# Multiplying constants before the gathered rows arrive, in two mixture-of-experts stages

## The reference

```python
def _L0_ffn_ref(x, ...):            # E = 32 experts, K = 4 per token, at most 320 rows each
    w, idx = _gate(xf, wg)
    xe = xp[buf_tok].reshape(E, cap, DIM)              # rows gathered by expert
    h = silu(einsum('ecd,edh->ech', xe, w1)) * einsum('ecd,edh->ech', xe, w3)
    out = einsum('ech,ehd->ecd', h, w2) * buf_w
    y = zeros.at[buf_tok].add(out)                     # rows sent home
    z = silu(xf @ sw1) * (xf @ sw3) @ sw2              # shared expert, every token
    return y + z

def _L3_ffn_ref(x, ...):            # 7 routed experts, 2 per token, one shared; hidden 512
    routed_out = _swiglu(x_flat, w_gate, w_up, w_down)
    mixed = einsum('end,ne->nd', routed_out, combine)
    return mixed + mean(_swiglu(x_flat, sw_gate, sw_up, sw_down), axis=0)
```

## Time and profile before

| | us |
|---|---|
| median of 3 runs | 1672.77 |
| lowest and highest | 1665.45, 1678.71 |
| profiled execution | 1683.69 |
| its span, first to last instruction | 1681.4 |
| TensorE busy | 1254.4 (75%) |
| VectorE busy | 1045.1 (62%) |
| ScalarE busy | 676.6 (40%) |
| GpSimd busy | 656.7 (39%) |

### The profile page before, as it was taken

How to read it: one execution, slowest core, us unless ns; L and a number is a source line. 1 busy time by engine, 2 the same in 40 slices (tenths; PEclk the granted TensorE clock), 3 DMA queues, 4 the chain that set the end, 5 groups by cost and what they waited for, 6 DMA issues and landing times.

```text
span 1681.4 us, 24800 instructions
## 1 busy us (share of the span) xinstructions
PE 1254.4 (75%) x9098; PEld 792.9 (47%) x9098; DVE 1045.1 (62%) x1915; ACT 676.6 (40%) x1275; POOL 656.7 (39%) x657
## 2 busy tenths in 40 slices
PE   5457777513777368878878559997998999965997
PEld 2123333311444134444446524454666666854996
DVE  7899999871211498878743454546665665642775
ACT  2744343210334137767741235554334234321442
POOL 1277878567366360000003330024641441043453
PEclk9679889856888579999968789998999999986998
DMA  6247567111232441211001141115000000001113
GB/s 221 103 161 258 212 233 267 55 43 49 70 81 67 151 145 39 64 57 44 16 15 31 44 154 54 38 35 220 1 1 1 1 1 1 1 31 40 37 47 95
DMA packets 75448, 133.84 MB, mean 80 GB/s; under 512 B 12723, under 2 KB 39670, under 8 KB 74688
## 3 DMA queue, kind: packets, MB, share of 16 engines
q1 hardware_dynamic: 66400, 115.97, 20.8%
q0 software_dynamic: 8064, 13.87, 2.6%
q10 hardware_dynamic: 864, 2.43, 0.4%
HBM read 96.22 MB, written 38.38 MB: 80 GB/s over the span
## 4 chain that ended last, share of the span: by engine, by line
PE 47%; issue 19%; DVE 13%; POOL 8%; ACT 5%; SPq 3%; DMA 3%; another core or an unknown queue 2%; POOLq 0%; DVEq 0%; ACTq 0%
PE ps L1840 6%; POOL sb_arena L1044 5%; PE ps L3956 3%; DVE sb_arena L1906 3%; PE ps L2207 2%; ACT sb_arena L2154 2%; PE ps L2190 2%; PE ps L2449 2%; PE ps L3115 2%; SPq L68 1%; PE ps L3131 1%; PE ps L658 1%; PE ps L3923 1%; PE ps L3924 1%
## 5 line engine op out<-in xcount | busy, mean ns | idle before, releaser
L1906 DVE TENSOR_REDUCE sb_arena<-ps 128x2 f32<-128x1024 f32 (+2 forms) x192 | 211.0, 1130 | 58.2 <-PE ps L2435 33.7
L2154 ACT ACTIVATE sb_arena<-ps 128x512 f32<-128x512 f32 (+1 forms) x320 | 160.3, 554 | 57.9 <-PE ps L2207 54.4
L658 PE MATMUL ps<-sb_arena,sb_const 128*128 128x512 f32 x256 | 136.1, 677 | 27.9 <-DVE sb_arena L852 27.9
L846 DVE TENSOR_TENSOR_SCAN sb_arena<-ps,sb_arena 128x1024 f32<-128x1024 f32 x64 | 145.0, 2279 | 4.0 <-ACT ps L945 3.1
L1938 POOL CAST sb_arena<-sb_arena 128x8 bf16<-128x8 f32 (+2 forms) x32 | 6.5, 203 | 289.4 <-DVE sb_arena L1906 148.8
L1840 PE MATMUL ps<-sb_arena 128*32 128x256 f32 (+3 forms) x1856 | 117.2, 361 | 0.2 <-ACT sb_arena L2388 0.2
L1566 POOL DMA_INDIRECT y<-sb_arena x80 | 77.7, 972 | 61.1 <-ACT sb_arena L1515 41.1
L658 PEld LDWEIGHTS ps<-sb_arena,sb_const 128*128 128x128 f32 x256 | 55.9, 220 | 93.1 <-issue 53.5
L1143 POOL DMA_INDIRECT xe<-sb_arena x80 | 78.5, 981 | 51.8 <-issue 29.2
L1044 POOL TENSOR_TENSOR sb_arena<-sb_Wreg,sb_arena 128x1024 f32<-128x1024 f32 x32 | 78.0, 2458 | 40.4 <-DMA sb_arena<-bcrows 32.2
L3776 POOL TENSOR_TENSOR sb_arena<-sb_arena 128x512 f32<-128x512 f32 x32 | 40.7, 1271 | 124.5 <-DVE sb_arena L3380 124.5
(11 more groups left out here) (519 smaller groups left out, 3233.7 us busy)
## 6 DMA issues: line engine op xcount, KB each, us to landing
sb_arena<-bcrows SPq DMA_DIRECT2D x80, 512.0 KB, 6.4
xe<-sb_one SPq DMA_DIRECT2D x31, 260.0 KB, 8.9
sb_Wreg<-e0w SPq DMA_DIRECT2D x24, 256.0 KB, 7.1
sb_arena<-xe SPq DMA_DIRECT2D x16, 325.0 KB
y<-sb_zero SPq DMA_DIRECT2D x20, 256.0 KB, 6.9
sb_arena<-y SPq DMA_DIRECT2D x4, 1024.0 KB, 9.3
sb_Wreg<-e1w SPq DMA_DIRECT2D x16, 256.0 KB, 2.7
sb_Wreg<-e3gu SPq DMA_DIRECT2D x1, 4096.0 KB, 12.5
```

Of the source, the lines that this page charges most:

```text
L658: t = e.matmul(k.b(self.Y + c), k.c("ident"), self.hc[i % 4][:, c * 512:(c + 1) * 512], start=False, stop=n == 15)
L846: e.tensor_tensor_scan(self.hh[i % 3], k.pair(2 * (i % 2)).rearrange("p c t -> p (c t)"), self.dB[i % 3], 0.0, MUL, ADD).then_inc(S.scan.s ...
L1906: e.tensor_reduce(dst, src, AX.X, MAX).then_inc(S.mxr.sem, 1)
L2154: e.activation(self.PT[s % 4][:, 2 * h:2 * h + 2, 0:n], bank[:, :, 0:n], ACT.Exp, scale=self.scale).then_inc(S.ex.sem, 1)
```

## The change

The last few scatters of each stage get a counter of their own. In the 32-expert stage the first 58 of 64 scatters add to the counter `row0` (whose later use, for the results sent home, starts from a base that is higher by as much), and the last 6 to `scat`. In the last stage it is the first 27 of 32, and the last 5. SyncE waits for both counters before the first load, so it still waits for all scatters. TensorE gets a wait for the first counter, and behind it a new helper, `spin_pe`: products of the identity matrix with other constants, written to a part of PSUM that nobody reads before it is written again. There are 8 of them with 512 columns in the 32-expert stage (bank 6), and 16 with 256 columns in the last stage (upper half of bank 5). All are float32.

```diff
@@ helper @@
+def spin_pe(k, e, out, n):
+
+    for _ in range(n):
+        e.matmul(out, k.c("ident"), k.const[:, 0:out.shape[-1]], start=True, stop=True)
@@ Dispatch.scatter @@
-    def scatter(self, e, w, buf, xn, rows, cleared, sig, h=0):
+    def scatter(self, e, w, buf, xn, rows, cleared, sig, h=0, ahead=None, until=0):
...
-                                     bounds_check=rows - 1, oob_is_err=False).then_inc(sig.sem, 16)
+                                     bounds_check=rows - 1, oob_is_err=False).then_inc((ahead if c < until else sig).sem, 16)
@@ Moe32 @@
+    AHEAD = 58
...
-            scat=1024, smg=4, smu=4, ssg=4, shs=4, sdn=4, sx=4,
+            scat=16 * (64 - self.AHEAD), smg=4, smu=4, ssg=4, shs=4, sdn=4, sx=4,
...
-            row0=480, row1=400, row2=400, back0=16, back1=16, back2=16, back3=16)
+            row0=480 + 16 * self.AHEAD, row1=400, row2=400, back0=16, back1=16, back2=16, back3=16)
+        self.ahead = S.row0
...
@@ Moe32.sp @@
-        w.wait_ge(S.scat, 1024)
+        w.wait_ge(self.ahead, 16 * self.AHEAD)
+        w.wait_ge(S.scat, 16 * (64 - self.AHEAD))
@@ Moe32.pe @@
         w.wait_ge(S.sx, 4)
         w.wait_ge(k.g_w["e0"], 384)
+        w.wait_ge(self.ahead, 16 * self.AHEAD)
+        spin_pe(k, e, k.b(6), 8)
         self.trans_pe(e, w, 0)
@@ Moe7 @@
-    BLK, NB, FRONT = 256, 22, 7
+    BLK, NB, FRONT, AHEAD = 256, 22, 7, 27
...
@@ Moe7.sp @@
-        w.wait_ge(S.scat, 512)
+        w.wait_ge(self.ahead, 16 * self.AHEAD)
+        w.wait_ge(S.scat, 16 * (32 - self.AHEAD))
@@ Moe7.pe @@
             if more and v < self.FRONT:
                 w.wait_ge(S.iw, 1)
+                w.wait_ge(self.ahead, 16 * self.AHEAD)
+                spin_pe(k, e, k.b(5)[:, 256:512], 16)
                 self.turn_pe(e, w, self.blocks[v + 1][1])
@@ Moe7.pool @@
-                                     bounds_check=self.ROWS - 1, oob_is_err=False).then_inc(S.scat.sem, 16)
+                                     bounds_check=self.ROWS - 1, oob_is_err=False).then_inc((self.ahead if c < self.AHEAD else S.scat).sem, 16)
```

## The result

The changed kernel took 1682.6 us (median of 17 runs, 1677.04 to 1688.51), the kernel before, beside it, 1674.99 us (17 runs, 1663.37 to 1683.59). The ratio is 1.0054, with a 95% interval of 1.0033 to 1.0074. The forecast was +14.1 us and 1686.9 us: the direction is right, the size is too large.

The account below looks back on a forecast made before the run. No engine is full; TensorE, busy for 75% of the span, comes late to both places. 6.9 + 7.2 = +14.1 us on the median of 1672.77 gives 1686.9 us, range 1666 to 1694.

Parts of the forecast that it names:

- The stall: Both stages: engines stand on "remote" under the scatters, 19.5 to 31.9 us, so TensorE comes later than the rows.
- Counters at 0: Both stages: splitting the scatters over two counters costs 0, since SyncE still waits for the same last scatter.
- Eight products: 32-expert stage: 8 products behind VectorE's last addition push the transposes by their full 6.9 us, through to the end.
- Rival C: Both stages: the products run exposed at the lower clock, 13.4 + 14.5 = +27.9 us, 1700.7; chance 0.06.
- Sixteen products: Last stage: 16 products start at 1553.2, where TensorE is the chain, and add 7.2 us to the end.
- Nothing is bought: Both places: the clock is already 1.00 ahead of the products, so a warm start gains nothing.
- Rival A: Both stages: products hidden ahead of the rows, warm start gains 2.45 us a stage, together 4.9: 1667.9; chance 0.20.
- B: A stall of half the length: products exposed in the last stage, hidden in the 32-expert stage, +4.8: 1677.5; chance 0.20.
- D: Both stages: the products are dropped or cost TensorE nothing, 1672.8; chance 0.06.

Follow-up runs that it names:

- nospin: The changed kernel without any products, counters and waits kept, on a chip showing nothing on "remote": 1623.42 us, ratio 1.0014 against the kernel before.
- nospin2: The changed kernel without any products, counters and waits kept, on a chip with the stall: 1672.08 us, ratio 0.9992 against the kernel before.
- early32: The changed kernel without last-stage products, its 32-expert products waiting for 40 scatters instead of 58: 1686.14 us, ratio 1.0032 against the kernel before.
- fit7: The changed kernel with the last stage waiting for 25 scatters instead of 27 and 22 products instead of 16: 1693.2 us, ratio 1.0078 against the kernel before.
- fit7b: The kernel with 25 scatters awaited and 22 products in the last stage, run once more: 1687.55 us, ratio 1.0088 against the kernel before.
- again: The changed kernel, untouched, on a chip showing nothing on "remote": 1617.44 us, ratio 0.9973 against the kernel before.

## Why the prediction was right, and where it was not

**The stall is in the timed runs: right, but the argument for it does not hold.** The prediction inferred it from a profiled execution that was only 5 to 18 us longer than the three others. Each timed run in the results comes with a span and a granted clock of its own, so the others may have been recorded as well, and then the comparison says nothing about the recorder. What the runs do show is that kernels before of 1672 to 1681 us go with profiles that have "remote", and kernels of 1622 to 1623 us with profiles that have none. "NOTIFIC — the notification-queue block", section 7.1, in the Trainium skill says that the pipeline inside the block that writes trace records holds its producers back rather than lose a record. That this makes the stall is neither confirmed nor refuted here: no execution is known to have run without the recorder.

**Counters at 0: right.** "nospin" gave +2.3 us (-1.0 to +5.5) and "nospin2" -1.3 us (-5.7 to +3.2).

**Eight products, 6.9 us, directly behind VectorE: right in place, short in length.** They took 7.13 us in "early32", but 8.83 in the changed kernel and in "fit7" and 8.69 in "fit7b", where a part of them ran at the lower clock. Rival C's clock was thus met for some of the records, not for all. The transposes came at 440.17 (forecast 441.4), 8.67 us behind the products' start.

**Sixteen products, 7.2 us, directly behind the down products: right.** 7.07 us, and the transposes 6.9 us after the products' start. They were forecast for 1567.3 and came at 1557.87, since all that lies ahead came 2.2 us earlier (1550.96 for 1553.20), and since the 6.9 us of the first stage did not arrive there. The profiles show where they went. The last result of the 32-expert stage went home 3.5 us later than in before (562.63 for 559.11). From there to the first scatter of the 8-expert stage, a stretch that no version changes, it is 319.5 us after and 325.0 before, and 316.5 to 325.0 in all fourteen profiles. So this stretch alone moves a span by up to 8.5 us from execution to execution, and the profile of before was its longest. The distance between two single spans can't be taken for the worth of the change.

**"Nothing is bought", since the clock is 1.00 ahead of both places: this step doesn't hold in general.** It took the clock of one execution, for that of all. In "nospin2" the experts of the 32-expert stage start at 0.50, and a warm start would be worth 7.09 - 4.25 = 2.8 us there. With it the profile's exposure of the change is 12.86 - 7.09 = 5.8 in the first stage (431.50 to 444.36 is 12.86) and 6.9 in the last, 12.7 us; without it 8.6 + 6.9 = 15.5. Measured were 9.0 (5.5 to 12.4). For "early32" the two sums are 4.1 and 6.9, measured 5.4; for "fit7" 15.3 and 18.1, measured 13.1, for "fit7b" 15.1 and 18.0, measured 14.7. If the kernel before mostly starts its experts cold in its timed runs, as "nospin2" does in its profile, a warm start accounts for the direction of the miss and about 3 of its 5 us. That it does was not shown: the one profile of before starts them warm. Of the four comparisons three lie below the smaller of their two sums and one between them, but only for the changed kernel does that sum, 12.7, lie outside the interval, and by 0.3 us. Shorter stalls in some of the timed runs could add to it; that was not shown either. So the part of the sum that did not hold is what the products buy, which was put at nothing; how much of the 5 us it accounts for stays open.

**Rival A, at 0.20, is what happens on the chips without the stall.** It gave 4.9 us of gain; measured 4.4. Of its parts, the waits were foreseen (TensorE free before the scatter, products hidden in the 32-expert stage), and the end of the last stage's products 2.0 us ahead of the rows was not met: they start at the lower clock, take 9.82 and not 7.2 us, and end about 1 us after them. The times of the rows were a little off as well: 3.1 us from load to transposes in the 32-expert stage and 2.5 in the last, where 2.77 was taken for both. "TensorE: Matmul & The Clock Gate", section on why this matters for your kernels, in the Trainium skill advises against idle gaps between bursts; "again" and "nospin" agree, with 3.2 and 2.6 us for the two gaps. On the chips with the stall there was no gap where the products came.

**Rivals B, C and D.** B (exposed in one stage) and C in full (all records at the lower clock, +27.9) fit none of the profiles after. The 14 us in B's sum 1520.2 + 14 are given without a source, and half of the stall of 31.9 us would be 16; either is past the rows, so +4.8 stands. D fell with the first one: the products are there, and the transposes wait for them.

## What to carry to other kernels

Work that is put into a gap is worth what the gap is on the chip that runs it: here one program gained 4.4 us with the gap and lost 9.0 us without it, and the bracket of the filling instruction (released by the scatter, or by VectorE) told the two apart. Before filling a wait, look whether something other than the awaited transfer makes the waiting engine late, and take the clock at the place from more than one execution. To see whether useful work is a better filling, look at what covers it where it stands now: the eighth shared block was already free.

## What was not expected of the hardware

One program's time differed by 49 to 59 us between chips (kernels before of 1622.25 and 1623.46 us on two, 1672.58 and 1681.14 us on two others), with the same instructions and nearly the same rhythm of scatters (39.7 to 39.8 us from the first to the last of the 32 with the stall, 39.8 to 40.3 without). "nospin" and "nospin2" are one program on a chip without the stall and on one with it, so their profiles tell where the time goes:

| start, us | nospin | nospin2 | later by |
|---|---|---|---|
| 32 experts: last scatter | 418.57 | 416.01 | -2.6 |
| last result sent home | 535.82 | 551.87 | 16.1 |
| 8 experts: first scatter | 856.66 | 871.89 | 15.2 |
| last result sent home | 912.15 | 937.67 | 25.5 |
| last stage: first scatter | 1444.90 | 1475.36 | 30.5 |
| first transposes | 1489.88 | 1540.41 | 50.5 |
| end of the span | 1620.7 | 1668.9 | 48.2 |

The 8-expert stage, which the change doesn't touch, and the sending home of the 32 experts' results (101 to 103 us without the stall and 116 to 119 with it, in all fourteen profiles) lose time as well. All the large steps lie in stretches in which GpSimd issues indirect DMAs. Under the scatters the timeline of the changed kernel, profiled beside the first result, shows TensorE finishing one record in up to 2.8 us:

```profile
1522.83 0.37 PE L3969 MATMUL ps<-sb_Wreg,sb_arena 128*128 128x128 f32 x1 [2.42 <-issue]
1525.62 0.37 PE L3969 MATMUL ps<-sb_Wreg,sb_arena 128*128 128x128 f32 x1 [2.43 <-issue]
```

while "again" has 16 records of the same line in one row of 1.95 us:

```profile
1471.16 1.95 PE L3969 MATMUL ps<-sb_Wreg,sb_arena 128*128 128x128 f32 x16
```

Each chip was seen on one occasion, so whether it is the chip or the occasion is open, and so is the cause. The clock of the changed kernel fell to 0.60 under the first products at 432 to 436 us, though TensorE had not been idle for more than 0.9 us at a time since 425.29; ahead of 423.42 it had been idle for 24.88 us.
